# Causal masks of the row maxima: from a TensorE mask product to a fused VectorE minimum, with whole-array turns of the maxima and a new order table

## What is computed

```
scores = q k^T * SCALE            # 256 x 256 per head
scores = where(causal, scores, -1e30)   # layer 0: key < query (row 0 keeps key 0); layer 1: key <= query
probs  = softmax(scores)
x      = x + (probs v) Wo ...
layer 0: ffn = x @ sign(W)         layer 1: 16 experts, top 2, and 2 shared experts
layer 2: quantised gated ffn       layer 3: three low-rank-corrected blocks with GELU
```

## Time and profile before

| | us |
|---|---|
| median of the three timed runs | 1257.43 |
| lowest and highest of them | 1252.65, 1260.58 |
| the profiled execution | 1244.47 |
| its span, first to last instruction | 1242.7 |

### The profile page before, as it was taken

The page is one execution under the profiler, slowest core; times in us unless marked ns, Lnnn a source line. Parts: engine busy times, 40 slices in busy tenths (PEclk is TensorE's granted clock), DMA queues, the critical chain, the costliest instruction groups (busy, mean ns, idle before and its releaser), DMA issues.

```text
span 1242.7 us, 25774 instructions
## 1 busy us (share of the span) xinstructions
PE 1116.6 (90%) x8662; PEld 801.7 (65%) x8662; DVE 915.3 (74%) x2503; ACT 826.6 (67%) x1558; POOL 551.0 (44%) x1089
## 2 busy tenths in 40 slices
PE   5999999999999986989999988779898998978987
PEld 4667777776887864766777655546565665545655
DVE  3678877676545566788757679898888988799643
ACT  5667656555666543666667647558879797887964
POOL 7132263666444374568763434224335232424244
PEclk9999999999999997999999999799999999999998
DMA  8764421323766542323396871231302221212000
GB/s 245 246 205 154 136 86 53 100 86 110 225 183 196 141 141 60 91 81 91 121 264 180 255 193 56 69 106 31 88 28 77 69 60 56 73 47 65 10 9 18
DMA packets 98353, 140.00 MB, mean 113 GB/s; under 512 B 12336, under 2 KB 79792, under 8 KB 98224
## 3 DMA queue, kind: packets, MB, share of 16 engines
q1 hardware_dynamic: 90192, 105.58, 29.1%
q0 software_dynamic: 8032, 32.78, 9.0%
HBM read 65.43 MB, written 22.54 MB: 71 GB/s over the span
## 4 chain that ended last, share of the span: by engine, by line
PE 54%; DVE 21%; ACT 11%; issue 7%; POOL 4%; DMA 2%; another core or an unknown queue 1%; SPq 0%; DVEq 0%; ACTq 0%; POOLq 0%
PE ps L1702 12%; PE ps L1826 5%; PE ps L1743 5%; PE ps L1722 5%; PE ps L1695 4%; DVE neg_max L2380 4%; PE ps L1918 4%; PE ps L1709 3%; ACT probs L2134 2%; ACT q_st L2149 2%; PE ps L1746 2%; DVE tri L2377 2%; PE ps L1725 2%; PE ps L1925 2%; DVE bn L2260 2%
## 5 line engine op out<-in xcount | busy, mean ns | idle before, releaser
L2134 ACT ACTIVATE probs<-ps 128x384 f32<-128x384 f32 (+1 forms) x512 | 264.7, 544 | 102.7 <-PE ps L1746 54.0
L1722 PE MATMUL ps<-k_st,q_st 96*128 96x256 bf16 (+1 forms) x1024 | 180.5, 263 | 35.1 <-DVE neg_max L2380 8.4
L1743 PE MATMUL ps<-q_st,k_st 104*128 104x256 bf16 (+1 forms) x1024 | 180.8, 265 | 13.8 <-ACT q_st L2149 6.9
L2377 DVE TENSOR_REDUCE tri<-ps 128x3 f32<-128x384 f32 x256 | 136.0, 550 | 62.8 <-PE ps L1725 52.9
L2380 DVE TENSOR_REDUCE neg_max<-ps 128x2 f32<-128x512 f32 x256 | 169.0, 681 | 16.9 <-PE ps L1722 10.3
L2149 ACT ACTIVATE q_st<-ps 8x1024 bf16<-8x1024 f32 x128 | 130.0, 1016 | 39.1 <-PE ps L1808 33.0
L1722 PEld LDWEIGHTS ps<-k_st,q_st 96*128 96x128 bf16 x1024 | 87.8, 99 | 89.5 <-DVE neg_max L2380 19.6
L1743 PEld LDWEIGHTS ps<-q_st,k_st 104*128 104x128 bf16 x1024 | 89.1, 99 | 70.9 <-issue 20.9
L1826 PE MATMUL ps<-probs,v 128*32 128x256 f32 (+1 forms) x2048 | 124.5, 361 | 4.1 <-ACT probs L2134 2.9
L2693 POOL TENSOR_SCALAR var_eps<-mv 128x2 f32<-128x2 f32 (+1 forms) x115 | 27.9, 243 | 221.2 <-DVE mv L2263 215.7
L2856 POOL DMA_INDIRECT w<-in_expert,w_row x62 | 62.2, 1003 | 102.3 <-PE ps L1925 67.0
(11 more groups left out here) (271 smaller groups left out, 2573.1 us busy)
## 6 DMA issues: line engine op xcount, KB each, us to landing
k_st<-parts SPq DMA_DIRECT2D x192, 128.0 KB
q_st<-parts SPq DMA_DIRECT2D x192, 128.0 KB
x_rows<-wo SPq DMA_DIRECT2D x10, 768.0 KB, 8.0
ctx_t<-in_ctx_t SPq DMA_DIRECT2D x16, 256.0 KB, 3.7
ring<-x_rows SPq DMA_DIRECT2D x31, 128.0 KB
y_rows<-ring SPq DMA_DIRECT2D x31, 128.0 KB
xn_t<-x_rows SPq DMA_DIRECT2D x31, 128.0 KB
y_rows<-vec SPq DMA_DIRECT2D x31, 128.0 KB
```

Source lines behind the costliest of these rows:

```text
L1722: last = mm(t[:, c0:c0 + n], head(q_st, r, h, KROWS, j * P, P), head(k_st, r, h, KROWS, 0, n), start=j == 0 or L == 3, stop=L == 3, skip_g ...
L1743: last = mm(t[:, j * S:j * S + n], head(k_st, r, h, KALL, j * P, P), head(q_st, r, h, KALL, skip, n), start=j == 0 or L == 3, stop=L == 3, ...
L2134: nc.scalar.activation(probs[:, (hg % 2) * HPG + h4, 0:width], tile_of(key)[:, 0:width], ACT.Exp, scale=SCALE).then_inc(*tile_drained(key))
L2377: V.tensor_reduce(tri[:, hg, h4, :], tile_of(key)[:, 0:3 * P].rearrange("p (j t) -> p j t", t=P), AX.X, ALU.max, negate=True).then_inc(*ti ...
```

## The change

It has four parts and a new table.

1. The mask matmul L1725 is gone. `reduce` does a causal head with two `tensor_tensor_reduce`, one for each half of the queries. The first takes 128 scores, the second 256, each adds a mask from SBUF, negates, takes the running minimum, and writes one value per partition to `neg_max`. The masked scores are written back to PSUM. In the built program each is an instruction over the scores and a further one that writes the single value. `diag_s` holds four blocks of 128, one of them zeros. `tri` and the step L2388 are gone. Only the second of the two frees the bank.
2. `max_parts` is widened with zeros from 8 to 104 columns, so that `turn_max` uses the whole array and needs no tile position. It has two buffers instead of four, and the writer waits for the turn two groups back.
3. `DRAIN` is 0.6 instead of 6: in the table's count a bank is free almost when its reader is placed.
4. The steps of the four head groups, which were lanes of each item, are six lanes over all items. A few waits are added where a buffer of the last layer's blocks is used again, and one for the weights of layer 2's values.
5. `AT` is another table.

```diff
-    (336, 339, 347, 352, 375, 389, 398, 401, 427, 443, 454, 459, 482, 496, 501, 509, 521, 535, 537, 548, 562, 593, 607, 609,
+    (336, 338, 347, 351, 372, 385, 390, 398, 419, 432, 437, 444, 460, 473, 476, 486, 508, 511, 519, 523, 541, 553, 556, 576,
...
-DRAIN = 6
+DRAIN = 0.6
...
-        diag_s = sb("diag_s", [P, 2, SJ, P], BF16)
+        diag_s = sb("diag_s", [P, 4, P], BF16)
...
-        max_parts = sb("max_parts", [P, HG, SJ, 2 * HPG], BF16)
+        max_parts = sb("max_parts", [P, 2, SJ, KALL], BF16)
...
-                              start=j == 0 or L == 3, stop=L == 3, skip_group_check=L < 3)
-                if CAUSAL[L]:
-                    last = mm(t[:, 0:2 * S].rearrange("p (j t) -> p j t", j=SJ)[:, :, 0:P], ident_b[:, :], diag_s[:, L, :, :],
-                              start=False, stop=True, skip_group_check=True)
-                elif L == 2:
+                              start=j == 0 or L != 2, stop=L != 2, skip_group_check=L == 2)
+                if L == 2:
...
-                        last = mm(t[KROWS:KALL, j * P:(j + 1) * P], max_parts[:, hg, j, :], ident_b[:, :],
-                                  start=True, stop=True, tile_position=(0, KROWS), skip_group_check=True)
+                        last = mm(t[0:KALL, j * P:(j + 1) * P], max_parts[:, hg % 2, j, :], ident_b[:, :],
+                                  start=True, stop=True, skip_group_check=True)
...
                     if CAUSAL[L]:
-                        V.tensor_reduce(tri[:, hg, h4, :], tile_of(key)[:, 0:3 * P].rearrange("p (j t) -> p j t", t=P),
-                                        AX.X, ALU.max, negate=True).then_inc(*tile_drained(key))
+                        for j, (c0, n0, step) in enumerate(((0, 3 * L, 1), (P, 1, 1 + L))):
+                            some = tile_of(key)[:, c0:c0 + (j + 1) * P].rearrange("p (j t) -> p j t", t=P)
+                            last = V.tensor_tensor_reduce(some, some, diag_s[:, n0:n0 + j * step + 1:step, :], -1.0, -NEG,
+                                                          ALU.add, ALU.min, neg_max[:, hg, h4, j:j + 1])
+                        last.then_inc(*tile_drained(key))
...
-                    if SLOT[L, b]:
-                        wait_filled(dve, ("t", *ORDER[SLOT[L, b] - 1], hg))
+                    if hg > 1:
+                        wait_filled(dve, ("t", L, b, hg - 2))
+                    elif SLOT[L, b]:
+                        wait_filled(dve, ("t", *ORDER[SLOT[L, b] - 1], hg + 2))
                     wait_drained(dve, key)
-                    if CAUSAL[L]:
-                        V.tensor_tensor(neg_max[:, hg, :, :], tri[:, hg, :, 0:SJ], tri[:, hg, :, 0:3:2], ALU.min).then_inc(
-                            *max_least.step((L, b, hg)))
-                        dve.wait_ge(*max_least.at((L, b, hg)))
...
+                    if n == 0:
+                        for before in same_set_before(b):
+                            wait_filled(dve, ("yt", NBLK - 1, before))
```

More of the change, by code:

```diff
@@ L899, in reductions, with max_turns, max_copies, weighted_values @@
             part.reduce(L, b, h)
-def max_rows(part, L, b, hg):
-    yield
-    part.turn_max(L, b, hg)
-    yield
-    part.rows(L, b, hg)
-def head_group(part, L, b, hg):
-    yield
-    part.values(L, b, hg)
-    yield
-    part.copy_output(L, b, hg)
-    yield
-    part.output(L, b, hg)
-    yield
-    part.normalise(L, b, hg)
+def max_turns(part):
+    for L, b in ORDER:
+        for hg in range(HG):
+            yield
+            part.turn_max(L, b, hg)
+def max_copies(part):
+    for L, b in ORDER:
+        for hg in range(HG):
+            yield
+            part.rows(L, b, hg)
+def weighted_values(part):
+    for L, b in ORDER:
+        for hg in range(HG):
+            yield
+            part.values(L, b, hg)
+def value_copies(part):
+    for L, b in ORDER:
+        for hg in range(HG):
+            yield
+            part.copy_output(L, b, hg)
+def value_turns(part):
+    for L, b in ORDER:
+        for hg in range(HG):
+            yield
+            part.output(L, b, hg)
+def value_shares(part):
+    for L, b in ORDER:
+        for hg in range(HG):
+            yield
+            part.normalise(L, b, hg)
 def keys(part, L, b):
@@ L1516, in y_set, with same_set_before @@
             return y_sets[1 if b in (B - 3, B - 1) else 0]
+        def same_set_before(b):
+            before = [c for c in range(b) if (c in (B - 3, B - 1)) == (b in (B - 3, B - 1))]
+            return before[-1:]
         def h_of(b):
@@ L1568, in claim @@
             for _ in range(IDLE.get(key, 0)):
-                nc.tensor.matmul(ps[:, bank, :], ident_b[:, :], diag_s[:, :, :, :].rearrange("p l j t -> p (l j t)"), start=True,
+                nc.tensor.matmul(ps[:, bank, :], ident_b[:, :], diag_s[:, :, :].rearrange("p n t -> p (n t)"), start=True,
                                  stop=True, skip_group_check=True)
@@ L1767, in token @@
                     t = claim(pe, (what, 2, b))
[L1768 removed]
+                    if what != "q":
                         pe.wait_ge(*load["w2nd"].at(0))
@@ L2228, in half_gelu @@
                     key = ("yt", n, LAST, a)
+                    if n == 0:
+                        for before in same_set_before(LAST):
+                            wait_filled(act, ("z", NBLK - 1, before))
                     wait_filled(act, key)
```

21 lines of the change are left out of this document (10 added, 11 removed), and 1284 rows, old and new, of the table AT.

## The result

| | before | changed |
|---|---|---|
| median of the timed runs, same chip, us | 1255.04 | 1209.15 |
| lowest and highest of them | 1247.78, 1260.58 | 1206.10, 1216.86 |
| the profiled execution | 1244.47 | 1206.10 |
| its span | 1242.7 | 1204.3 |
| exponential of head 256 (the last causal one) ends, from the span's start | 556.8 | 541.4 |

The ratio is 0.9647 (95% interval 0.9576 to 0.9718). The change is worth 3.5 to 4%, 44 to 51 us, where 18 were forecast. The median before has here a fourth run that the table ahead of the prediction had not.

A forecast was written before the change was run, and what follows sets the result against it. TensorE was taken to set the first half's pace with VectorE behind it, the later half being shared. Terms -21, -12 and +15 us sum to -18, giving 1239 us from 1257.43; own range 1222 to 1250, 8-in-10 range 1216 to 1268.

The forecast's parts named there:

- The table and `DRAIN`: Bank choice and instruction order: smaller `DRAIN` cuts loans of maxima banks from 83 to 23, unpriced; counted as nothing.
- the new order as a whole: Order of steps over the whole kernel: taken as nothing, with 8 us either way.
- The mask matmul: Causal stretch: removing 256 mask matmuls frees 28 us of TensorE, three quarters of it counting by the chain: -21 us.
- The fused minimum: Causal heads on VectorE: 0.69 us a head instead of 0.46, 46 us more work, a third counting: +15 us.
- The turn: Turns of the maxima on TensorE: gaps of 0.09 and 0.10 us go, 9 us causal plus 3 later: -12 us.
- The sum: Whole kernel: -21 - 12 + 15 = -18 us, giving 1239 us, 1.4% faster.
- The signs to look for: Causal stretch ending at 525 to 535 us, turn starts 0.11 us apart, a head's four instructions starting within 0.7 us.
- VectorE becomes the bound: Rival, causal stretch: at 0.90 us a head VectorE needs 539 us, +21 us, 1278 us; chance of slower 0.18.
- Given back: Rival, later stretch: the first half's 15 us gain is lost there, 14 us lost, 1253 us; chance 0.26.
- Relief in full: Rival, mainly causal stretch: all 28 + 12 us of TensorE count and VectorE stays hidden, 1214 us; chance 0.10.

The follow-up runs named there:

- the spare matmul: A 256-column matmul, overwritten by the scores, added per causal head: kernel before 1.0164; before with fused minimum 1.0064; changed kernel 0.9703, all against the kernel before.
- the one with no loans: Changed kernel with `DRAIN` 0.6, other steps forbidden to borrow a PSUM bank of the maxima, against the kernel before: ratio 0.9757.

## Why the prediction was wrong

**The table and `DRAIN` (the step that failed).** The prediction listed the smaller `DRAIN` with "no row prices it" and took "the new order as a whole" as nothing, 8 us either way. Measured, `DRAIN` alone is worth 2.1% (26 us) and the table 0.5 to 1.5%. Of the 4.0% in all, parts 1 and 2 hold 0.55% if they are made first and 1.5% if last, so the table and `DRAIN` hold 62 to 86%, in the one place where the sum had a zero. By stage it shows in the heads 257 to 320, which took 209 us before and take 188 now. On the old table parts 1 and 2 leave them at 209, and the new table without parts 1 and 2 has them at 189. The loans had been counted (83 to 23), and the price could have been bounded from the waits of the kernel before over the whole span:

```profile
PEld ps L1722 <- DVE neg_max L2380: 19.6, 39, 2.9
PEld ps L1722 <- DVE tri L2377: 15.9, 25, 2.2
...
PE ps L1722 <- DVE neg_max L2380: 8.4, 15, 2.7
PE ps L1722 <- DVE tri L2377: 7.3, 10, 1.7
```

TensorE's weight loads wait 35 us for the reductions of both kinds of heads, and the longest waits, 2.2 to 2.9 us, are four to five times what a reduction takes (0.46 to 0.68 us). What is longer than one reduction can lie in the choice of the bank. That bound, a gain of 0 to some 35 us, was left out, and so the range ended at 1216. It is a bound and no account: of the 35 us only 12 went with `DRAIN` 0.6. The clock, with which 7 to 11 of the 26 us go, stood in no term either.

**The mask matmul (mis-sized).** 28 us of TensorE's time is right: the spare matmul of the same size takes it by starts. The share of three quarters, from the chain, holds for work that is added to the kernel before: 20 us. With the fused minimum in place it was worth 11 to 13 us, two fifths to a half. The chain prices the kernel as it stands; once the fused minimum is in and the matmul goes, the next limit is close (the waits for VectorE and its banks). No run takes the matmul away with VectorE's work unchanged, so it isn't shown which of the two lowers its worth.

**The fused minimum (mis-sized twice).** The price of a head was 0.59 us (0.58 to 0.63), not 0.69. The two reads of the accumulator, taken as 0.08 each, cost nothing, but for the 0.24 us at the end of a group. The 256-value operation took 0.38 instead of 0.33. So VectorE gained 20 us of busy time on the page and 0.13 x 256 - 13 = 20 us by starts, where 46 were forecast. Of these more counted than the third that was taken: 8 to 10 of 20 us, so too low a share and too high a price met in the term. The term comes out at 8 to 10 where it said 15. What is late is as it was said: the bank is held for 0.21 + 0.38 + 0.14 = 0.73 us instead of 0.55, and TensorE's waits for it on the old table rose from 7.3 to 21.4 us on PE. With `DRAIN` 0.6 the same waits are 7.7 us on the old table and 7.7 and 10.3 in two traces of the changed kernel.

**The turn (gaps right, worth mis-sized).** Both gaps were there, 0.09 and 0.10 us, and both went. That a turn beside the products of the values keeps a gap was right too: before, the mask matmul L1725 and the L1826 behind it start 0.20 us apart in 21 cases, where 0.11 is the rule. The relief is 0.2% on the old table, and 0.2% when it comes last on the new one: 2 to 3 us where 12 were forecast. Half of what TensorE saved (13 us of busy time) went into longer waits for the maxima's banks. But with the mask matmul still there, on the new table, it brought 1.2%. So its worth depends on what else has been taken away. At these sizes the intervals, 0.3 to 0.4%, are as large as the relief itself.

**The sum.** The terms of parts 1 and 2 were -21, +15 and -12, together -18. Measured on the old table they are -11, +8 and -3, together -6 (7 us when run together). Two errors of size nearly cancelled in part 1. On the old table parts 1 and 2 do not reach the total of -18. On the new one they take 1.5%, 18 us: that this meets the forecast is luck, since either part alone gives most of it, which no term of the sum foresees. The rest of the gain is the table's and `DRAIN`'s.

**The signs to look for.** The last causal exponential came 15 us earlier, inside the 10 to 20 forecast. That is no proof of the terms: with `DRAIN` 0.6 alone, on a chip nearly as fast, it ends at 543.8, 13 us earlier, with the mask matmul and the strip turns kept. The starts at the turn were 0.12 and 0.11 us, as forecast. A head's instructions start within 0.59 us (0.7). DVE busy in the causal stretch is 387 of 500 us (forecast about 400). TensorE's weight loads wait for DVE 16.1 us (forecast 25). The later stretch was to lose 3 us and lost 23.

**The rivals.** "VectorE becomes the bound" fell with the 0.59 us per head. The Trainium skill, "VectorE: DVE Perf Modes", section The DRAIN you can't avoid, says that the next operation starts only when the pipe is empty. It also says, which the prediction left out, that one that is not held starts earlier. The trace agrees with the second: of 1024 operations of L2193 all but 34 start before the end of the one ahead, and those 34 had waited. The price of 0.90 us per head in that rival is also not the middle of the upper half of 0.69 to 1.01, which is 0.93; nothing hangs on it. "Given back" was wrong in sign: the order gained. "Relief in full" had a number near the result (1214), but its mechanism is not what happened, since TensorE's relief did not count in full.

**What stays open.** Why parts 1 and 2 are worth two to three times as much on the new table, and why either of them alone gives nearly all of it. The waits don't tell: with `DRAIN` 0.6, parts 1 and 2 raise PE's waits for the causal maxima alike on both, from 1.1 to 7.7 us on the old and from 3.0 to 7.7 or 10.3 on the new. The clock may hold a part of it, but its noise in the changed kernel is too large to tell. Which of the moved steps carries the table's own gain wasn't tried; the six lanes and the added waits came with the table and weren't tried apart either. And `DRAIN` changes the number of loans and the choice among banks together, in every run here, the one with no loans (0.9757) included.

## What to carry to other kernels

A constant that only decides which buffer is taken can be worth more than an edit that removes work: look at the longest waits for a buffer, compare them with how long its reader takes, and price the surplus before calling a new placement nothing. The chain's share of an operation priced the added matmul rightly here; of the one that was replaced by work on another engine only half arrived. And when an edit relieves the leading engine, ask at once which shared resource (here two PSUM banks) it will be waiting for next. Compare the mean granted clock of the executions too: a gain in waits and a gain in clock look alike in the time.

## What the hardware showed

A fused add and minimum over PSUM with its result written back costs VectorE 0.21 us for 128 values (0.25 in most heads that follow another at once) and 0.38 for 256, from start to start. The read of its accumulator into SBUF is an instruction of its own with 0.14 us in the trace. After 414 of the 512 reads the next operation starts with it, so there it costs no throughput; the cast that needs the value starts 0.24 us after the read's start. A turn on an 8-column strip between whole-array matmuls costs 0.09 us ahead and 0.10 behind, which 104 columns avoid. A matmul of 256 columns in bfloat16 is followed after 0.11 us at 2.4 GHz and after 0.21 at 1.2. The Trainium skill, "TensorEngine Tiling (Array Packing)", section Key Properties, has the drain behind this; the trace agrees.
